# Attention on one NeuronCore: where p_low is made, and how the products for the row maxima are laid into TensorE

## The chip, the cores and the metric

One NeuronCore of one Trainium2 chip. The metric is the device time of one execution in microseconds. Engines: PE (TensorE, with PEld for its weight loads), DVE (VectorE), ACT (ScalarE), POOL (GpSimd), SP (SyncE, here the DMA queue).

## The reference

x is (2, 16, 128, 1024), that is 2 batches of 2048 tokens of 1024 channels, float32. It is group-normalized, goes through masked attention with 16 heads of 64 dimensions, 8 that look back and 8 that look ahead, and an output projection, and is added to x:

```python
def _masked_attention(xf, Wq, Wk, Wv, lookahead):
    q, k, v = (einsum('bnd,hed->bhne', xf, W) for W in (Wq, Wk, Wv))
    s = einsum('bhqe,bhke->bhqk', q, k) / sqrt(64)
    s = where(mask, s, finfo.min)        # i >= j, or i <= j for lookahead
    p = softmax(s)
    return einsum('bhqk,bhke->bhqe', p, v)
o = concatenate([o_lb, o_la], axis=1).reshape(B, T * F, D)
return x + einsum('bnd,od->bno', o, Wo)
```

## The kernel before

Float32 accuracy is had from products of the type fp32r: every operand is split in a rounded high part and a low part (the rest), and two or three products are added. A first stage, to about 1110 us, makes q, k and v of all heads (project) and stores them. The second, attend, goes over 32 heads one after the other, two (p = 0, 1) in a turn of a loop.

A head has four stages of 512 queries and 40 score tiles of 128 keys by up to 512 queries. Tiles above the diagonal are left out, so stage s has 4s full tiles and four diagonal ones of 512, 384, 256 and 128 columns. The number of such a diagonal tile modulo 4 is 0, 1, 2, 3 in that order. The shift of the softmax is a maximum over q_high times k of each query, made beforehand in 40 units (max_unit) of 128 queries by up to 512 keys, with the same counts of columns.

The order of the work is written out by hand in slots(): 40 slots a head, and each engine runs the same list and takes its own part. In slot t come: the product for the maxima of unit t+23 (of the next head past 40), the scores of tile t+3, diagonal and shift (the maxima laid on a diagonal, summed by PE into "side", copied into a row of q2), the steps of the division by the sums (invert, spread, divide, in three slots from 1, 9, 14 and 26 on), the splits of the next head's q, k and v (high parts on ACT, low parts on POOL in slots 1, 3, ... 19), the projection of the head before (8 matmuls in each of slots 9, 10, 11, 15, 16, 17), and the values of tile t.

The chain of a score tile: PE adds the products k1 q1 and k2 q2 (L1037, L1042, with a mask product L1040 on diagonal tiles) in one of two banks; ACT takes exp into probs (L859) and again, rounded, into p_high (L863); p_low = probs - p_high (L690) is made in two column parts, 3/8 on DVE and 5/8 on POOL; PE adds three products with v (L1056, L1058, L1060). probs, p_high and p_low have four buffers each. DVE makes its part of tile n-1 at the scores step of tile n. PE waits for both parts before the values, and ACT before it overwrites probs.

Partitions 0 to 63 of q1 and 64 to 127 of it both hold q_high. k1 holds k_high over k_low. k2 holds k_high in rows 0 to 63, ones in row 64 and zeros below; q2 holds q_low in rows 0 to 63 and in row 64 the shift. So k1 q1 + k2 q2 is the shifted score.

The product for the maxima (L1012) is k1 q1 over 128 rows into one of two banks by turns; PE waits until DVE has read the unit two before. DVE adds a mask to diagonal units (L921) and reduces (L927); minus_max (L932) closes a stage.

Of the kernel before, what the change touches and what calls it, by code (L numbers as in the profile page):

```python
# [5 lines left out]
F32 = mybir.dt.float32  # L6
# [26 lines left out]
def reached(eng, sem, value):  # L33

    if isinstance(value, int) and value <= 0:
        return
    eng.wait_ge(sem, value)
# [407 lines left out]
ROUND_SLOT = {("high", 0): 4, ("high", 1): 5, ("low", 0): 6, ("low", 1): 7}  # L445
OP_SLOT = {0: 9, 1: 10, 2: 11, 3: 15, 4: 16, 5: 17}
ADD_SLOT = {0: 13, 1: 19}
LOW_DVE = (3, 8)
WO_UNITS = 16
WO_SLOT = {w: 12 + 3 * w // 2 for w in range(WO_UNITS)}  # L450

# [87 lines left out]
def attend(nc, x_res, wo, qk_s, v_s, out):  # L539
    with ExitStack() as ctx:  # L540
# [135 lines left out]

        def wait_low(eng, i, p, n):

            reached(eng, low_dve, count(i, p, S_TILES, n + 1))
            reached(eng, low_pool, count(i, p, S_TILES, n + 1))  # L680

        def low_part(eng, done, kind, i, p, n):

            cols = score_tile(kind, n % S_TILES)[5]
            mine = cols * LOW_DVE[0] // LOW_DVE[1]
            part = slice(0, mine) if done is low_dve else slice(mine, cols)
            wait_high(eng, i, p, n)

            reached(eng, weighed, count(i, p, S_TILES, n - 3))
            eng.tensor_tensor(p_low[:, n % 4, part], probs[:, n % 4, part],  # L690
                              p_high[:, n % 4, part].bitcast(F32), ALU.subtract).then_inc(done, 1)
# [14 lines left out]
        def split_low(eng, p, slot, u, h):  # L706

            src = slice(h * NQ, (h + 1) * NQ)
            cols = slice((u % 2) * HALF + h * NQ, (u % 2) * HALF + (h + 1) * NQ)
            if u < 2:  # L710
                ins = eng.tensor_tensor(q2[0:E, p, cols], raw[0:E, slot, src],
                                        q1[0:E, p, cols].bitcast(F32), ALU.subtract)
            elif u < 4:
                low = k1[E:P, p, cols]
                ins = eng.tensor_tensor(low, raw[E:P, slot, src], low.bitcast(F32), ALU.subtract)  # L715
            else:
                js = slice(h * TOK // 2, (h + 1) * TOK // 2)
                ins = eng.tensor_tensor(  # L718
                    v[:, p, js, 2 * E:3 * E], raw[:, slot, src].rearrange("p (t e) -> p t e", e=E),
                    v[:, p, js, 0:E].bitcast(F32), ALU.subtract)  # L720
            ins.then_inc(low_split, 1)
# [58 lines left out]
        @block.gpsimd  # L780
        def _(pool):
            nc.gpsimd.memset(eye[:, :], 0.0).then_inc(eye_made, 1)
            nc.gpsimd.memset(below[:, :], 0.0).then_inc(eye_made, 1)
            nc.gpsimd.memset(beyond[:, :], 0.0).then_inc(eye_made, 1)
            pool.wait_ge(eye_made, 3)
            nc.gpsimd.affine_select(out=eye[:, :], in_=eye[:, :], compare_op=ALU.not_equal, fill=1.0,
                                    base=0, pattern=[[-1, P]], channel_multiplier=1).then_inc(eye_made, 1)

            nc.gpsimd.affine_select(out=below[:, :], in_=below[:, :], compare_op=ALU.is_ge, fill=MASKED,
                                    base=0, pattern=[[1, P]], channel_multiplier=-1).then_inc(consts, 1)  # L790
            nc.gpsimd.affine_select(out=beyond[:, :], in_=beyond[:, :], compare_op=ALU.is_ge, fill=MASKED,
                                    base=0, pattern=[[-1, P]], channel_multiplier=1).then_inc(consts, 1)

            pool.wait_ge(consts, 2)
            for p in range(2):
                nc.gpsimd.memset(q2[E:P, p, :].bitcast(F32), 0.0).then_inc(cleared, 1)
                nc.gpsimd.memset(k2[E:P, p, :].bitcast(F32), 0.0).then_inc(cleared, 1)  # L800
            pool.wait_ge(cleared, 4)
            for p in range(2):
                nc.gpsimd.memset(k2[E:E + 1, p, :].bitcast(F32), 1.0).then_inc(cleared, 1)
            pool.wait_ge(cleared, 6)
            for p in range(2):
                nc.gpsimd.memset(v[:, p, :, E:2 * E].bitcast(F32), 1.0).then_inc(cleared, 1)
                nc.gpsimd.memset(v[:, p, :, 3 * E:VC].bitcast(F32), 0.0).then_inc(cleared, 1)

            def do(step, kind, i, p, n):
                if step == "split low" and not first_head(i, p):  # L810

                    u, h = n // 2, n % 2
                    slot = (p * RAW_UNITS + u) % 2
                    pool.wait_ge(act_split, count(i, p, SPLITS, n + 1))


                    reached(pool, low_split, count(i, p, SPLITS, n))
                    reached(pool, low_pool, count(i, p, S_TILES, LOW_SLOT[n] + AHEAD - S_TILES + 1))
                    split_low(pool, p, slot, u, h)
                    pool.wait_ge(low_split, count(i, p, SPLITS, n + 1))  # L820
                elif step == "scores":
                    low_part(pool, low_pool, kind, i, p, n)

            heads(pool, do)

        @block.scalar
        def _(act):
            def do(step, kind, i, p, n):
                if step in ("split high", "k2 high"):
# [7 lines left out]
                    cols = slice((u % 2) * HALF + h * NQ, (u % 2) * HALF + (h + 1) * NQ)  # L837
                    if step == "k2 high":

                        nc.scalar.activation(k2[0:E, p, cols], raw[0:E, slot, src], ACT.Copy)  # L840
                    elif u < 4:
                        nc.scalar.activation((q1 if u < 2 else k1)[:, p, cols], raw[:, slot, src],
                                             ACT.Copy).then_inc(act_split, 1)
                    else:
                        js = slice(h * TOK // 2, (h + 1) * TOK // 2)
                        nc.scalar.activation(v[:, p, js, 0:E], raw[:, slot, src].rearrange(
                            "p (t e) -> p t e", e=E), ACT.Copy).then_inc(act_split, 1)
                elif step == "shift":

                    act.wait_ge(row_ready, count(i, p, STAGES, n + 1))  # L850
                    qb = n if kind == LB else STAGES - 1 - n
                    nc.scalar.activation(q2[E:E + 1, p, qb * NQ:(qb + 1) * NQ], side[E:E + 1, :],
                                         ACT.Copy).then_inc(shift_ready, 1)
                elif step == "scores":
                    cols = score_tile(kind, n)[5]
# [30 lines left out]
        def _(dve):  # L886
# [14 lines left out]
            def both_parts(kind, i, p, n):  # L901

                if n % 4 in HIGH_DVE:
# [3 lines left out]
                    reached(dve, weighed, count(i, p, S_TILES, n - 3))  # L907
                    nc.vector.tensor_copy(p_high[:, n % 4, 0:cols],
                                          probs[:, n % 4, 0:cols]).then_inc(high_dve, 1)
                low_part(dve, low_dve, kind, i, p, n)  # L910

            def do(step, kind, i, p, n):
                if step == "diagonal":
# [86 lines left out]
        def _(pe):  # L1000
            pe.wait_ge(consts, 3)

            def do(step, kind, i, p, n):
                if step == "max":
                    _, _, _, qc, key, cols, _ = max_unit(kind, n)
                    if n == 0:

                        pe.wait_ge(low_split, count(i, p, SPLITS, 8))

                    reached(pe, max_read, count(i, p, M_UNITS, n - 1))  # L1010
                    to = max_bank[n % 2]
                    nc.tensor.matmul(to[:, 0:cols], q1[:, p, qc * P:(qc + 1) * P],  # L1012
                                     k1[:, p, key:key + cols], start=True, stop=True).then_inc(max_scored, 1)
                elif step == "shift":
                    if first_head(i, p) and n == 0:

# [104 lines left out]
```

## Time and profile before

| what | value |
|---|---|
| median of 3 runs | 3432.36 us (3430.88 to 3432.69) |
| span of the profiled execution | 3431.4 us |
| PE, DVE, ACT, POOL busy | 3164.0, 2272.0, 1744.9, 1542.0 us |
| attention alone, 1300 to 3300 us: PE, DVE, ACT, POOL busy | 1862.55, 1816.54, 1425.80, 1338.35 us |

A matmul's end is modelled, and the next one begins before it: a row of 0.39 us does not mean that the next begins 0.39 us later; the starts tell the pace. The granted clock is that of TensorE, 1.00 for the full one. "Idle before" is the time that an engine stood still before an instruction, and the releaser is what ended it.

### The profile page before, as it was taken

The numbers are of one execution on the slowest core, as the hardware profiler recorded it, in microseconds if no ns is written. First come the engines' busy times: TensorE is split into PE (matmuls) and PEld (weight loads), VectorE is DVE, ScalarE is ACT, GpSimd is POOL, SyncE is SP. The second block draws the span as 40 slices with busy tenths as digits, with TensorE's granted clock in tenths as the row PEclk, the third lists the DMA queues.
The fourth block names the chain that finished last, engine by engine and source line by source line (L and its number), as shares of the span: only waits on it lengthen the run. The fifth ranks groups of instructions, "written<-read, shape, count | busy, mean of one in ns | idle before, by whom it ended". The sixth has DMA issues, their size and how long they took to land.

```text
span 3431.4 us, 53634 instructions
## 1 busy us (share of the span) xinstructions
PE 3164.0 (92%) x14472; PEld 2465.1 (72%) x14472; DVE 2272.0 (66%) x4412; ACT 1744.9 (51%) x3525; POOL 1542.0 (45%) x1626
## 2 busy tenths in 40 slices
PE   4999998999999589989999999999998999999998
PEld 3888887788888367767766677677776777767766
DVE  6212111310110599998998989998999899898996
ACT  2100101210100377777677777677777767776775
POOL 2000000100000466666666666676766666666663
PEclk9999999999999699999999999999999999999999
DMA  6234213422312222111121112111211112111210
GB/s 233 98 90 131 92 64 95 138 73 50 97 60 49 74 80 68 45 50 52 53 62 44 55 50 68 44 50 56 61 51 50 50 51 67 44 49 56 63 36 19
DMA packets 142566, 233.09 MB, mean 68 GB/s; under 512 B 76800, under 2 KB 76800, under 8 KB 142336
## 3 DMA queue, kind: packets, MB, share of 16 engines
q1 hardware_dynamic: 142336, 230.73, 22.3%
q14 instruction: 172, 1.41, 0.1%
q8 instruction: 58, 0.95, 0.1%
HBM read 163.58 MB, written 67.11 MB: 67 GB/s over the span
## 4 chain that ended last, share of the span: by engine, by line
PE 27%; DVE 13%; issue 13%; POOL 8%; ACT 4%; DMA 1%; POOLq 0%; DVEq 0%; ACTq 0%; SPq 0%
PE rows L1074 6%; POOL p_low L690 4%; PE max L1012 4%; DVE part_max L927 3%; PE scores L1042 3%; PE acc L1056 3%; PE acc L1060 3%; PE acc L1058 3%; DVE p_low L690 3%; PE scores L1037 3%; DVE o_full L981 2%; POOL k L715 2%; ACT p_high L863 2%; POOL v L718 2%; DVE inv L967 1%
## 5 line engine op out<-in xcount | busy, mean ns | idle before, releaser
L690 POOL TENSOR_TENSOR p_low<-probs,p_high 128x320 fp32r<-128x320 f32 (+3 forms) x1280 | 1072.6, 845 | 740.7 <-ACT p_high L863 678.9
L859 ACT ACTIVATE probs<-scores 128x512 f32<-128x512 f32 (+3 forms) x1280 | 686.6, 536 | 524.9 <-PE scores L1042 499.3
L927 DVE TENSOR_REDUCE part_max<-max 128x1 f32<-128x512 f32 (+3 forms) x1280 | 766.0, 599 | 83.2 <-PE max L1012 62.6
L863 ACT ACTIVATE p_high<-scores 128x512 fp32r<-128x512 f32 (+3 forms) x1280 | 685.6, 536 | 0.0
L1012 PE MATMUL max<-k,q 128*128 128x512 f32 (+3 forms) x1280 | 493.7, 387 | 164.7 <-DVE part_max L927 142.7
L690 DVE TENSOR_TENSOR p_low<-probs,p_high 128x192 fp32r<-128x192 f32 (+3 forms) x1280 | 634.2, 496 | 16.1 <-ACT p_high L863 14.2
L318 DVE COPY stage_d<-proj 128x512 f32<-128x512 f32 x96 | 66.0, 689 | 710.9 <-PE proj L264 461.1
L1042 PE MATMUL scores<-q,k 128*128 128x512 f32 (+3 forms) x1280 | 510.0, 398 | 0.0
L1056 PE MATMUL acc<-p_high,v 128*128 128x512 f32 (+3 forms) x1280 | 476.2, 372 | 9.4 <-issue 6.4
L1037 PE MATMUL scores<-q,k 128*128 128x512 f32 (+3 forms) x1280 | 475.2, 371 | 4.4 <-ACT p_high L863 4.3
L1060 PE MATMUL acc<-p_low,v 128*128 128x512 f32 (+3 forms) x1280 | 473.3, 370 | 0.0
L1058 PE MATMUL acc<-p_high,v 128*65 128x512 f32 (+3 forms) x1280 | 467.0, 365 | 0.0
L1012 PEld LDWEIGHTS max<-k,q 128*128 128x128 f32 x1280 | 247.3, 193 | 261.9 <-DVE part_max L927 203.4
L318 ACT COPY stage_a<-proj 128x512 f32<-128x512 f32 x96 | 56.0, 586 | 682.2 <-PE proj L264 359.6
L264 PE MATMUL proj<-xh,wh 128*128 128x512 f32 x896 | 348.8, 389 | 0.0
L264 PE MATMUL proj<-xh,wl 128*128 128x512 f32 x896 | 348.6, 389 | 0.0
L264 PE MATMUL proj<-xl,wh 128*128 128x512 f32 x896 | 348.6, 389 | 0.0
L1060 PEld LDWEIGHTS acc<-p_low,v 128*128 128x128 f32 x1280 | 244.9, 191 | 93.3 <-issue 5.0
L206 POOL TENSOR_TENSOR xl<-xs,xh 128x1024 fp32r<-128x1024 f32 x16 | 42.1, 2635 | 588.7 <-ACT xh L362 588.7
L1056 PEld LDWEIGHTS acc<-p_high,v 128*128 128x128 f32 x1280 | 246.5, 193 | 56.2 <-issue 18.9
L1037 PEld LDWEIGHTS scores<-q,k 128*128 128x128 f32 x1280 | 245.0, 191 | 46.1 <-ACT p_high L863 8.6
L1042 PEld LDWEIGHTS scores<-q,k 128*128 128x128 f32 x1280 | 251.7, 197 | 25.2
(94 smaller groups left out, 4981.7 us busy)
## 6 DMA issues: line engine op xcount, KB each, us to landing
raw<-qk_s SPq DMA_DIRECT2D x256, 256.0 KB, 4.2
xs<-xT SPq DMA_DIRECT2D x64, 512.0 KB, 4.8
w_raw<-wqk SPq DMA_DIRECT2D x32, 512.0 KB, 3.6
qk_s<-stage_a SPq DMA_DIRECT2D x64, 256.0 KB, 2.4
qk_s<-stage_d SPq DMA_DIRECT2D x64, 256.0 KB, 2.4
raw<-v_s SPq DMA_DIRECT2D x64, 256.0 KB, 2.8
res<-x_res SPq DMA_DIRECT2D x32, 512.0 KB, 4.1
out<-res SPq DMA_DIRECT2D x32, 512.0 KB, 2.6
```

What stands on the lines that cost most here:

```text
L264: last = nc.tensor.matmul(bank[4 * u + q][:, :], w[:, u, c, :], x[:, c, cols], start=(c == 0 and w is wh and x is xh), stop=(c == NC - 1 a ...
L690: eng.tensor_tensor(p_low[:, n % 4, part], probs[:, n % 4, part], p_high[:, n % 4, part].bitcast(F32), ALU.subtract).then_inc(done, 1)
L859: nc.scalar.activation(probs[:, n % 4, 0:cols], scores[n % 2][:, 0:cols], ACT.Exp, scale=SCALE).then_inc(exp_done, 1)
L863: nc.scalar.activation(p_high[:, n % 4, 0:cols], scores[n % 2][:, 0:cols], ACT.Exp, scale=SCALE).then_inc(high_act, 1)
L927: nc.vector.tensor_reduce(part_max[:, s % 2, at, m:m + 1], max_bank[n % 2][:, 0:cols], AX.X, ALU.max).then_inc(max_read, 1)
L1012: nc.tensor.matmul(to[:, 0:cols], q1[:, p, qc * P:(qc + 1) * P], k1[:, p, key:key + cols], start=True, stop=True).then_inc(max_scored, 1)
L1037: nc.tensor.matmul(to[:, 0:cols], k1[:, p, keys], q1[:, p, queries], start=True, stop=False)
L1042: nc.tensor.matmul(to[:, 0:cols], k2[:, p, keys], q2[:, p, queries], start=False, stop=True).then_inc(scored, 1)
L1056: nc.tensor.matmul(sums[:, col:col + cols], v[:, p, j, 0:P], high, start=first, stop=False, skip_group_check=True)
L1058: nc.tensor.matmul(sums[0:E + 1, col:col + cols], v[:, p, j, P:VC], high, start=False, stop=False, skip_group_check=True)
L1060: nc.tensor.matmul(sums[:, col:col + cols], v[:, p, j, 0:P], low, start=False, stop=final, skip_group_check=True).then_inc(weighed, 1)
L1074: last = nc.tensor.matmul(rows_bank[:, :], o[:, j, :], w[:, j, cols], start=(k == 0), stop=(k == 23))
```

## The change

p_low of a tile is made whole by one engine: by DVE for tiles with n % 4 = 3, by POOL for the others. The waits follow the counts of the one engine concerned.

q2 and k2 are turned over: k2 has ones in row 0, zeros in rows 1 to 63 and k_high in rows 64 to 127; q2 has the shift in row 0 and q_low in rows 64 to 127. The products for the maxima are issued two at a time, at even n: unit n on rows 0 to 63 (q1 and k1), unit n+1 on rows 64 to 127 (q1 and k2), each into its own bank. Their maximum is now over q_high k_high without k_low; it only shifts the softmax. PE waits before a pair until DVE has read all units up to n-1.

```diff
-LOW_DVE = (3, 8)
+LOW_DVE = (3,)
+LOW_POOL = (0, 1, 2)
...
         def wait_low(eng, i, p, n):
-            reached(eng, low_dve, count(i, p, S_TILES, n + 1))
-            reached(eng, low_pool, count(i, p, S_TILES, n + 1))
+            if n % 4 in LOW_DVE:
+                wait_one(eng, low_dve, LOW_DVE, i, p, n)
+            else:
+                wait_one(eng, low_pool, LOW_POOL, i, p, n)
         def low_part(eng, done, kind, i, p, n):
-            cols = score_tile(kind, n % S_TILES)[5]
-            mine = cols * LOW_DVE[0] // LOW_DVE[1]
-            part = slice(0, mine) if done is low_dve else slice(mine, cols)
+            part = slice(0, score_tile(kind, n % S_TILES)[5])
...
             if u < 2:
-                ins = eng.tensor_tensor(q2[0:E, p, cols], raw[0:E, slot, src],
-                                        q1[0:E, p, cols].bitcast(F32), ALU.subtract)
+                ins = eng.tensor_tensor(q2[E:P, p, cols], raw[E:P, slot, src],
+                                        q1[E:P, p, cols].bitcast(F32), ALU.subtract)
...
-                    reached(pool, low_pool, count(i, p, S_TILES, LOW_SLOT[n] + AHEAD - S_TILES + 1))
+                    wait_one(pool, low_pool, LOW_POOL, i, p, LOW_SLOT[n] + AHEAD - S_TILES)
...
-                elif step == "scores":
+                elif step == "scores" and n % 4 in LOW_POOL:
                     low_part(pool, low_pool, kind, i, p, n)
...
-                        nc.scalar.activation(k2[0:E, p, cols], raw[0:E, slot, src], ACT.Copy)
+                        nc.scalar.activation(k2[E:P, p, cols], raw[E:P, slot, src], ACT.Copy)
...
-                low_part(dve, low_dve, kind, i, p, n)
+                if n % 4 in LOW_DVE:
+                    low_part(dve, low_dve, kind, i, p, n)
...
-                if step == "max":
-                    _, _, _, qc, key, cols, _ = max_unit(kind, n)
+                if step == "max" and n % 2 == 0:
...
-                    reached(pe, max_read, count(i, p, M_UNITS, n - 1))
-                    to = max_bank[n % 2]
-                    nc.tensor.matmul(to[:, 0:cols], q1[:, p, qc * P:(qc + 1) * P],
-                                     k1[:, p, key:key + cols], start=True, stop=True).then_inc(max_scored, 1)
+                    reached(pe, max_read, count(i, p, M_UNITS, n))
+                    for m, part, keys in ((n, slice(0, E), k1), (n + 1, slice(E, P), k2)):
+                        _, _, _, qc, key, cols, _ = max_unit(kind, m)
+                        nc.tensor.matmul(max_bank[m % 2][:, 0:cols], q1[part, p, qc * P:(qc + 1) * P],
+                                         keys[part, p, key:key + cols], start=True, stop=True).then_inc(max_scored, 1)
```

The memsets of q2 and k2 and the copy of the shift move to the other rows with them.

## Rows read from the trace of the kernel before

**Rows 1.** The page's first part: busy us (share of the span) xinstructions.

```profile
PE 3164.0 (92%) x14472; PEld 2465.1 (72%) x14472; DVE 2272.0 (66%) x4412; ACT 1744.9 (51%) x3525; POOL 1542.0 (45%) x1626
```

**Rows 2.** Busy by stretch: us, PE, PEld, DVE, ACT, POOL (x), PEclk, DMA share, GB/s.

```profile
1300.00:3300.00 2000.00, 1862.55 (x8805) 1415.14 (x8804) 1816.54 (x3665) 1425.80 (x2982) 1338.35 (x1432) 0.99 0.18 53
2020.62:2037.43 16.81, 12.23 (x55) 7.69 (x53) 14.75 (x26) 12.29 (x28) 10.59 (x12) 1.00 0.12 33
2037.43:2063.32 25.89, 25.62 (x119) 20.36 (x120) 22.41 (x46) 16.31 (x34) 18.25 (x18) 1.00 0.13 41
2063.32:2091.90 28.58, 27.27 (x138) 20.83 (x137) 26.97 (x61) 21.67 (x47) 18.17 (x23) 1.00 0.26 74
...
2024.70:2041.20 16.50, 13.21 (x58) 8.45 (x57) 16.32 (x28) 12.97 (x28) 13.35 (x13) 1.00 0.12 33
```

**Rows 3.** Waits, 1300 to 3300: engine line waited for: total us, times, longest.

```profile
POOL p_low L690 <- ACT p_high L863: 565.2, 598, 3.6
...
PE max L1012 <- DVE part_max L927: 119.0, 108, 2.3
DVE max L921 <- PE max L1012: 73.8, 112, 1.6
...
ACT k L840 <- DMA raw<-qk_s: 39.1, 28, 3.0
DVE max L921 <- issue: 22.2, 10, 2.5
```

**Rows 4.** Timeline of PE, slot 31: start, us, instruction [idle before it].

```profile
2007.86 0.33 PE L1012 MATMUL max<-k,q 128*128 128x128 f32 x1 [1.32 <-DVE part_max L927]
2008.03 0.45 PE L1037 MATMUL scores<-q,k 128*128 128x512 f32 x1
2008.31 0.40 PE L1042 MATMUL scores<-q,k 128*128 128x512 f32 x1
2008.55 0.39 PE L1056 MATMUL acc<-p_high,v 128*128 128x512 f32 x1
2008.78 0.39 PE L1058 MATMUL acc<-p_high,v 128*65 128x512 f32 x1
```

**Rows 5.** The page's costliest groups: xcount | busy, mean ns | idle before, releaser.

```profile
L690 POOL TENSOR_TENSOR p_low<-probs,p_high 128x320 fp32r<-128x320 f32 (+3 forms) x1280 | 1072.6, 845 | 740.7 <-ACT p_high L863 678.9
...
L690 DVE TENSOR_TENSOR p_low<-probs,p_high 128x192 fp32r<-128x192 f32 (+3 forms) x1280 | 634.2, 496 | 16.1 <-ACT p_high L863 14.2
```

**Rows 6.** Groups by form, 1300 to 3300 us, columns as in Rows 5.

```profile
L690 POOL TENSOR_TENSOR p_low<-probs,p_high 128x320 fp32r<-128x320 f32 x802 | 762.8, 958 | 523.4 <-ACT p_high L863 497.9 <-POOL k L715 11.2 <-POOL q L711 10.3
...
L690 DVE TENSOR_TENSOR p_low<-probs,p_high 128x192 fp32r<-128x192 f32 x802 | 452.9, 565 | 0.9 <-issue 0.3
...
L981 DVE TENSOR_TENSOR o_full<-acc_s,inv 64x256 f32<-64x256 f32 x228 | 210.4, 923 | 1.5
...
L711 POOL TENSOR_TENSOR q<-raw,q 64x512 fp32r<-64x512 f32 x116 | 163.8, 1412 | 15.0 <-POOL p_low L690 9.1 <-ACT k L842 0.2 <-ACT p_high L863 0.2
L715 POOL TENSOR_TENSOR k<-raw,k 64x512 fp32r<-64x512 f32 x113 | 148.3, 1313 | 14.8 <-POOL p_low L690 9.5 <-ACT k L842 1.5
...
L718 POOL TENSOR_TENSOR v<-raw,v 128x512 fp32r<-128x512 f32 x56 | 67.2, 1200 | 7.3 <-POOL p_low L690 5.4
...
L690 POOL TENSOR_TENSOR p_low<-probs,p_high 128x80 fp32r<-128x80 f32 x115 | 41.6, 362 | 45.2 <-ACT p_high L863 33.1 <-POOL v L718 6.0 <-POOL q L711 5.3
L690 DVE TENSOR_TENSOR p_low<-probs,p_high 128x144 fp32r<-128x144 f32 x115 | 41.3, 359 | 0.0
```

**Rows 7.** Timeline of DVE before the first head: a k split, POOL idle.

```profile
1138.59 0.69 DVE L715 TENSOR_TENSOR k<-raw,k 64x512 fp32r<-64x512 f32 x1 [0.35 <-ACT k L842]
```

**Rows 8.** Timeline of DVE: p_low without and with POOL busy.

```profile
2002.55 0.34 DVE L690 TENSOR_TENSOR p_low<-probs,p_high 128x192 fp32r<-128x192 f32 x1
...
2026.19 1.45 DVE L690 TENSOR_TENSOR p_low<-probs,p_high 128x192 fp32r<-128x192 f32 x1
```

**Rows 9.** Line 690 alone, DVE's stretch A: DVE busy, POOL busy, PEclk, DMA.

```profile
2024.70:2041.20 16.50, 6.43 (x9) 7.53 (x9) 1.00 0.12 33
```

More of the change, by code:

```diff
@@ L798, in _ @@
             for p in range(2):
-                nc.gpsimd.memset(q2[E:P, p, :].bitcast(F32), 0.0).then_inc(cleared, 1)
-                nc.gpsimd.memset(k2[E:P, p, :].bitcast(F32), 0.0).then_inc(cleared, 1)
+                nc.gpsimd.memset(q2[0:E, p, :].bitcast(F32), 0.0).then_inc(cleared, 1)
+                nc.gpsimd.memset(k2[0:E, p, :].bitcast(F32), 0.0).then_inc(cleared, 1)
             pool.wait_ge(cleared, 4)
             for p in range(2):
-                nc.gpsimd.memset(k2[E:E + 1, p, :].bitcast(F32), 1.0).then_inc(cleared, 1)
+                nc.gpsimd.memset(k2[0:1, p, :].bitcast(F32), 1.0).then_inc(cleared, 1)
             pool.wait_ge(cleared, 6)
@@ L851, in do @@
                     qb = n if kind == LB else STAGES - 1 - n
-                    nc.scalar.activation(q2[E:E + 1, p, qb * NQ:(qb + 1) * NQ], side[E:E + 1, :],
+                    nc.scalar.activation(q2[0:1, p, qb * NQ:(qb + 1) * NQ], side[0:1, :],
                                          ACT.Copy).then_inc(shift_ready, 1)
```

## The prediction

> **What bounds the kernel now.** I read the busy shares first [rows 1]: PE 92%, DVE 66%. They mix two stages. The diff touches only attention, so I read the steady stretch of attention next, 1300 to 3300 us [rows 2]: PE 1862.55 of 2000 us, DVE 1816.54, POOL 1338.35. Two engines near 91 to 93% means that they take turns, and the waits say how [rows 3]: PE stands waiting for DVE's reduction of the maxima (119.0 us in 108 times, its weight loads with it), DVE at other times for PE's product (73.8 us before the mask alone), POOL 565.2 us for ACT's p_high. o_full (L981) has 8 instructions a head, and 228 of them in 2000 us are 28.5 heads: 70.2 us a head, 32 heads. The sum below is made per head. The profiled execution's span is 3431.4 us, 1.0 under the median of the runs.
>
> Within one head [rows 2] I cut at PE's products for the maxima: A, slots 1 to 8 (16.81 us), B, slots 9 to 19, which hold the output projection (25.89 us), C, slots 20 to 39 and 0 (28.58 us). One matmul of 512 columns follows another after 0.23 us [rows 4], 0.45 ns a column. Columns by score_tile and max_unit: a head has 17408 for the maxima, twice that for scores, three times for values, 24576 for the projection and 2048 for the side rows. With 0.08 us for each of 16 masked tiles (my estimate) PE needs about 9.6 us in A, 25.0 in B, 25.8 in C: 60.4 of 70.2. So PE is held up mostly in A (7.2 us), 0.9 in B, 2.8 in C. DVE also waits now and then 2.2 us for nothing that the trace shows (22.2 us in 10 times, [rows 3]), at the loop's turn: 0.8 us a head, and I keep it.
>
> **Part 1: p_low whole, a tile on one engine.** Now each tile costs one DVE and one POOL instruction: 634.2 and 1072.6 us [rows 5], 19.8 and 33.5 us a head. The diagonal tiles sit at n%4 = 0 to 3 with 512, 384, 256, 128 columns, so DVE (n%4 = 3) gets 6 tiles of 512 and 4 of 128, POOL 22 of 512, 4 of 384 and 4 of 256.
> DVE: a tile of 128 columns costs no more than the 144 columns' 0.359 us [rows 6]; no tile of 512 is there. Lower end 0.69 us, a two-input DVE instruction of 512 columns with POOL idle [rows 7]; upper end 0.69 times 0.565/0.34 = 1.15 us, the slowing that p_low of 192 columns shows beside POOL (0.34 alone, 1.45 at worst, mean 565 ns, [rows 6, 8]). I take 0.9, in between, since POOL will be busy beside it most of the time. Sum 6 x 0.9 + 4 x 0.33 = 6.7 us a head: DVE loses 13.1 us of work.
> POOL: from 80 to 320 columns it goes from 362 to 958 ns [rows 6], 2.48 ns a column. 512 columns: 1.43 us by that slope; lower end 1.20, the v split of 128 x 512. I take 1.43, the same instruction at the same contention. 384 and 256 columns: 1.12 and 0.80. Sum 31.5 + 4.5 + 3.2 = 39.2, 5.7 us more than now. With ten splits (4 x 1.412 + 4 x 1.313 + 2 x 1.200 = 13.3 us [rows 6]) and some 0.4 us of hand-over around each, 56 us a head: below the period, but dense in A.
> A rule of the skill speaks against this. The slope on POOL (2.48 ns a column, [rows 6]) is over twice DVE's (512 columns in 0.69 us, [rows 7]). The Trainium skill (GPSIMD Engine Reference, Specifications and Instruction dispatch) puts the floor for two inputs at about 2.5 cycles an element of 1.2 GHz, an estimated 1.07 us for 512 columns, and says that VectorE is the place for such work; with 1.07 POOL's sum would be 8 us smaller, and nothing below would change, since POOL is not what I count as late.
>
> Stretch A, now. DVE is busy all of 2024.7 to 2041.2: 16.32 us, 6.43 of it p_low [rows 2, 9]. The rest, 9.9, stays; p_low becomes one tile of 512 and one of 128: 1.2. That is 11.1 us plus a second of waiting: the divide lands in slot 3 (two o_full of 0.92 us each [rows 6], a transpose, a diagonal around them), and PE can't go on. Before, the product of unit n waited for the read of n-2; now a pair waits for the read of n-1, so PE is one slot ahead of DVE at a pair, not two. Step by step, from the start of slot 1, with the durations of the rows and 0.6 us for a reduce: DVE reads unit 25 by 2.7 (a reduce and the invert before it), so the pair of slot 3 starts at 2.8, where PE alone would be there at 2.4. Then come a reduce, the divide of 2.1 and unit 27 with its mask: 6.7, and the pair of slot 5 starts at 6.8 where PE would be there at 5.2. Diagonal, two reduces and one p_low of 0.9: 9.4, the pair of slot 7 at 9.5. Two reduces, a mask and two o_low: 12.3, the pair of slot 9 at 12.4. That is A: 12.4 us, with 2.8 us of waits in it. POOL has there 4 tiles of 512, one of 384, one of 256 and four q splits with hand-over: 5.7 + 1.9 + 5.6 + 1.6 = 14.8 us, but what PE needs in A is only up to tile 8, 11.3 us after A's start. So POOL is just not late. With the loop's bubble A is 13.2 us.
> B: PE's own 25.0 and 0.3 for a hiccup. POOL's later splits delay the next raw load, which already holds up ACT now and then (39.1 us in 28 times, [rows 3]); the projection's 8 matmuls in three slots cover it (1.85 us each), otherwise it would cost 1 to 2 us a head.
> C: 25.8 and a stall of 1.3 that stands there now [rows 4]: the divide in slots 26 to 28 keeps its length; p_low takes less of it, but PE has one slot less of lead. 27.1 us.
> Sum, PE's work unchanged: 13.2 + 25.3 + 27.1 = 65.6 us a head against 70.2.
>
> **Part 2: maxima two at a time.** One pair takes rows 0 to 63 and 64 to 127 of the array and two banks. If the halves run at once, a pair lasts as long as its longer unit: 768 + 2048 + 3072 + 4096 = 9984 columns a head for 17408, 0.225 us a pair where two units took 0.392, 20 pairs a head. The trace holds no matmul on 64 rows, so this is bounded: below, 0.225 and free, -0.17 us a pair; above, no overlap and a full emptying of the array on both sides of the pair. The nearest row to an emptied array is a restart after a stall: the matmul of 128 columns is followed after 0.17 us where its columns take 0.06, 0.11 us extra [rows 4]. And a matmul shows 0.39 us where the next follows after 0.23: 0.16 us of tail. I take one restart at each change of shape and no tail: 0.225 + 0.22 = 0.445, +0.05 us a pair. In A DVE hides it; 16 pairs a head pay, +0.8 us. Reduces and masks on DVE don't change. The copies that moved from the lower to the upper rows, the memsets and the constants have the same shapes: nothing.
> Before the first head, DVE reads 23 units at some 20 us in all; without the second unit in flight each of 11 pairs shows some 0.4 us more: +4 us, once.
>
> **Sum.** 65.6 + 0.8 = 66.4 us a head; (66.4 - 70.2) x 32 = -122, + 4: 3431.4 - 118 = 3314 us in the profile's time, and one more by the median. I forecast 3315.
>
> **The rivals.**
> Free switching. PE takes the columns alone: 16 x (-0.17) = -2.7, of which DVE, one slot behind, gives back 0.4: 63.3 us a head, 3216 us. For: the weight loads lie under matmuls now. Against: nothing in the trace shows it.
> The Trainium skill (TensorEngine Tiling, Theoretical Speedup) gives up to 2x for 64 rows, which is this case.
> Emptying on both sides. Tail and restart, 2 x (0.16 + 0.11) = 0.54 us, on 0.225: 0.765 for 0.392, +0.37 us a pair. A absorbs its four; 16 x 0.37 = 5.9 on 65.6 makes 71.5 us a head: (71.5 - 70.2) x 32 + 4, so 3478 us, slower. It decides from +0.28 us a pair on: below, the kernel is faster. Without overlap of the halves it is 0.17 more, 74.2 us and 3564.
> Here the Trainium skill speaks against the change as well: TensorEngine Tiling, Key Properties, says that changing the tiling mode drains TensorE, and each pair changes it twice. No run here shows the price.
> A middle of that, +0.2 us a pair: 68.8 us a head, 3392 us.
> POOL becomes the bound. If a tile costs more than 1.43 because DVE's longer instructions hold it up, A follows POOL: 14.8 + 0.8 for 13.2, 68.8 us a head, again 3392. For: POOL would have almost no gap in slots 1 to 8. Against: ring and lead of three tiles.
> The split alone does nothing: if DVE's relief were not on PE's path, 70.2 + 0.8, 3462. Against: of PE's waits that have a releaser almost all end with DVE's reduction [rows 3].
>
> **How the numbers follow.** The forecast case (3286 to 3350) 0.38; free switching (3200 to 3286) 0.27; middle or POOL (3350 to 3424) 0.17; both-sided emptying and slower cases (above 3439) 0.15; in between, near no change, 0.03. Faster by over 0.2% (about what can be told from no change) 0.82, within 0.03, slower 0.15. The range leaves out the lower tail (0.05) and the worst of the emptying (0.12): 3215 to 3450.
>
> **What would show it.** Part 1: L690 on DVE x320 near 0.75 us mean and on POOL x960 near 1.3; POOL's busy share over 50% and DVE's under 62%; PE's waits for part_max under half. If A is late by POOL, p_low on POOL stands as the releaser of acc (L1056). Part 2: the two L1012 of a pair start within some tens of ns if the halves overlap; the gap from a pair to the scores matmul, less 0.23, is the price of switching. o_full x8 a head gives the new period: 66.4 is right, 71 or more means emptying, under 64 free switching. I am wrong first of all if a 64-row matmul or its weight load has a length of its own that no row here hints at.

## The result

The changed kernel takes 3617.35 us (median of 4 runs, 3613.84 to 3618.52), the kernel before 3431.62 in the same session: 1.0542 times as long, 95% interval 1.0527 to 1.0557. That is 186 us more where the prediction had 117 less. None of its rivals reached this time; the worst of them, emptying without overlap of the halves, was 3564. Over 32 heads it is 5.8 us a head. The profiled execution's span is 3615.3 us.

The page of the kernel after, busy time by engine (to be held against [rows 1]), and busy time by stretch with the columns of [rows 2]: the steady stretch of attention, then one head cut at the pairs of slots 1, 9, 21 and 1.

```profile
PE 3299.4 (91%) x14472; PEld 2388.9 (66%) x14472; DVE 2021.0 (56%) x3452; ACT 1760.1 (49%) x3525; POOL 1644.8 (45%) x1306
```

```profile
1300.00:3300.00 2000.00, 1849.77 (x8206) 1253.64 (x8205) 1472.13 (x2612) 1337.69 (x2764) 1330.18 (x1064) 0.96 0.17 50
...
2031.90:2046.56 14.66, 11.27 (x54) 7.21 (x53) 14.03 (x21) 11.46 (x25) 11.91 (x10) 1.00 0.12 36
2046.56:2074.81 28.25, 27.98 (x125) 20.00 (x126) 19.39 (x36) 18.66 (x36) 20.06 (x18) 1.00 0.13 39
2074.81:2107.00 32.19, 28.00 (x132) 18.37 (x132) 22.19 (x43) 20.21 (x44) 18.74 (x16) 0.99 0.22 65
```

DVE did lose its work: 1472 us of 2000 where it had 1816.54 [rows 2], and its 30 instructions fewer a head. But PE is no less busy, it does fewer heads in the time (8206 matmuls for 8805), and DVE, with time to spare, now waits for PE too. The waits, with the columns of [rows 3], and the groups by form, with those of [rows 6]:

```profile
DVE part_max L929 <- PE max L1014: 341.1, 287, 3.1
PEld max L1014 <- DVE part_max L929: 242.2, 244, 3.0
PE max L1014 <- DVE part_max L929: 143.2, 104, 2.5
```

```profile
L691 POOL TENSOR_TENSOR p_low<-probs,p_high 128x512 fp32r<-128x512 f32 x588 | 784.1, 1344 | 617.2 <-ACT p_high L864 563.6 <-PE acc L1062 36.3 <-POOL k L716 6.1
...
L983 DVE TENSOR_TENSOR o_full<-acc_s,inv 64x256 f32<-64x256 f32 x214 | 226.9, 1060 | 2.9 <-issue 1.5
...
L691 DVE TENSOR_TENSOR p_low<-probs,p_high 128x512 fp32r<-128x512 f32 x161 | 151.0, 938 | 0.0
```

PE waits for the reduction of the maxima more than before (143.2 us for 119.0), although DVE has less to do: two engines that wait for each other, neither full. 214 o_full are 26.75 heads in 2000 us, 74.8 us a head for 70.2.

The pair itself stands in the timeline of PE and, below it, of PE's weight loads, the kernel after, slot 13 and its neighbours (start, us):

```profile
2056.45 0.40 PE L1060 MATMUL acc<-p_high,v 128*65 128x512 f32 x1
2056.69 0.40 PE L1062 MATMUL acc<-p_low,v 128*128 128x512 f32 x1
2057.01 0.50 PE L1014 MATMUL max<-k,q 64*128 64x512 f32 x2
2057.44 0.51 PE L1039 MATMUL scores<-q,k 128*128 128x512 f32 x1
2057.78 0.40 PE L1044 MATMUL scores<-q,k 128*128 128x512 f32 x1
```

```profile
2056.45 0.19 PEld L1062 LDWEIGHTS acc<-p_low,v 128*128 128x128 f32 x1
2057.01 0.19 PEld L1014 LDWEIGHTS max<-k,q 64*128 64x128 f32 x2 [0.37 <-issue]
2057.44 0.19 PEld L1039 LDWEIGHTS scores<-q,k 128*128 128x128 f32 x1 [0.24 <-issue]
2057.55 0.19 PEld L1044 LDWEIGHTS scores<-q,k 128*128 128x128 f32 x1
```

Both products are one row with 0.50 us: they start within a hundredth of a microsecond of each other and run at once. Around them time is lost. A matmul of 512 columns is followed after 0.23 us elsewhere; here the pair starts 0.32 us after the last values matmul (0.09 more), the scores matmul 0.43 us after the pair (0.20 more), and the next 0.34 us after that (0.11 more). From the starts in the timeline from 1300 to 2300 us the medians are 0.10 (136 pairs without another wait), 0.43 (213) and 0.11 (120). The weight loads show the same places: the load of the last values matmul starts 0.24 us ahead of it (2056.45 for 2056.69), but the load of the 64-row products starts with them, and so does that of the first 128-row product behind them. A pair of full units costs 0.64 us where two products cost 0.46. Three gaps, some 0.40 us, stand against 7424 columns saved in 20 pairs, 0.17 us each.

### The profile page after: what moved, and what is told of

It is laid out like the page before. It is cut to its first block, busy times and chain, and to the rows that moved or that the text cites. A ratio compares the mean times of both kernels' runs of the same rounds, so it can differ in the third digit from the quotient of the medians.

```text
span 3615.3 us, 50218 instructions
## 1 busy us (share of the span) xinstructions
PE 3299.4 (91%) x14472; PEld 2388.9 (66%) x14472; DVE 2021.0 (56%) x3452; ACT 1760.1 (49%) x3525; POOL 1644.8 (45%) x1306
## 4 chain that ended last, share of the span: by engine, by line
PE 32%; POOL 12%; DVE 11%; issue 10%; ACT 1%; DMA 0%; POOLq 0%; DVEq 0%; SPq 0%; ACTq 0%
POOL p_low L691 6%; PE scores L1039 6%; PE max L1014 5%; PE rows L1076 5%; PE scores L1044 4%; PE acc L1062 4%; PE acc L1058 4%; PE acc L1060 4%; DVE part_max L929 3%; POOL k L716 3%; DVE p_low L691 3%; POOL q L712 2%; DVE o_full L983 2%; DVE inv L962 1%; DVE inv L969 1%
## 5 line engine op out<-in xcount | busy, mean ns | idle before, releaser
L691 POOL TENSOR_TENSOR p_low<-probs,p_high 128x512 fp32r<-128x512 f32 (+2 forms) x960 | 1168.1, 1230 | 831.8 <-ACT p_high L864 754.1
L1039 PE MATMUL scores<-q,k 128*128 128x512 f32 (+3 forms) x1280 | 554.4, 433 | 2.5 <-ACT p_high L864 2.3
L1014 PE MATMUL max<-k,q 64*128 64x512 f32 (+3 forms) x1280 | 327.0, 478 | 233.1 <-DVE part_max L929 201.7
L1044 PE MATMUL scores<-q,k 128*128 128x512 f32 (+3 forms) x1280 | 524.0, 409 | 0.0
L1062 PE MATMUL acc<-p_low,v 128*128 128x512 f32 (+3 forms) x1280 | 484.2, 378 | 0.0
L1060 PE MATMUL acc<-p_high,v 128*65 128x512 f32 (+3 forms) x1280 | 477.0, 373 | 0.0
L1014 PEld LDWEIGHTS max<-k,q 64*128 64x128 f32 x1280 | 123.6, 190 | 460.8 <-DVE part_max L929 325.7
L1039 PEld LDWEIGHTS scores<-q,k 128*128 128x128 f32 x1280 | 250.3, 196 | 176.7 <-issue 119.8
L1058 PEld LDWEIGHTS acc<-p_high,v 128*128 128x128 f32 x1280 | 253.8, 198 | 41.1 <-POOL p_low L691 2.2
L983 DVE TENSOR_TENSOR o_full<-acc_s,inv 64x256 f32<-64x256 f32 x256 | 269.2, 1051 | 3.6 <-issue 1.8
L1044 PEld LDWEIGHTS scores<-q,k 128*128 128x128 f32 x1280 | 260.6, 204 | 9.6
```

The lines of the kernel that those rows point to most:

```text
L983: last = nc.vector.tensor_tensor(o_full[a * E:(a + 1) * E, :, rows], sums, by, ALU.mult)
L1014: nc.tensor.matmul(max_bank[m % 2][:, 0:cols], q1[part, p, qc * P:(qc + 1) * P], keys[part, p, key:key + cols], start=True, stop=True).the ...
L1039: nc.tensor.matmul(to[:, 0:cols], k1[:, p, keys], q1[:, p, queries], start=True, stop=False)
L1044: nc.tensor.matmul(to[:, 0:cols], k2[:, p, keys], q2[:, p, queries], start=False, stop=True).then_inc(scored, 1)
L1058: nc.tensor.matmul(sums[:, col:col + cols], v[:, p, j, 0:P], high, start=first, stop=False, skip_group_check=True)
L1060: nc.tensor.matmul(sums[0:E + 1, col:col + cols], v[:, p, j, P:VC], high, start=False, stop=False, skip_group_check=True)
```

## The experiments

Four kernels take the change apart. Theories: S, the changes of the array's shape cost, from 128 rows to 64 for the products for the maxima and back; L, PE's lost lead costs: before a pair DVE must have read both banks, so PE can't be two slots ahead; P, whole tiles cost. A ratio is to the kernel before, measured again in the same session.

**The split alone.** The changed kernel with the products of before:

```diff
-                if step == "max" and n % 2 == 0:
+                if step == "max":
...
-                    reached(pe, max_read, count(i, p, M_UNITS, n))
-                    for m, part, keys in ((n, slice(0, E), k1), (n + 1, slice(E, P), k2)):
...
+                    reached(pe, max_read, count(i, p, M_UNITS, n - 1))
+                    to = max_bank[n % 2]
+                    nc.tensor.matmul(to[:, 0:cols], q1[:, p, qc * P:(qc + 1) * P],
+                                     k1[:, p, key:key + cols], start=True, stop=True).then_inc(max_scored, 1)
```

> Part 1 alone: p_low whole tiles on one engine as in the changed kernel, but the products for the maxima one at a time over 128 rows, waiting for the read of n-2. Theory S (the shape of the array is what costs: 0.63 us for a pair of 64-row products with its surroundings where two 128-row products take 0.46, so some 4 to 5 us a head): this kernel is faster than before, 65.6 us a head by the prediction's own sum, 3285 us, at any rate under 3400. Theory L (what costs is that PE is only one slot ahead of DVE at a pair): also under 3400. Theory P (whole tiles on POOL cost: DVE's o_full beside a 512-column POOL instruction rose from 0.92 to 1.05 us and to 1.5 at worst): at or above 3431.

Measured 3390.11 us, 0.9881 of before (0.9865 to 0.9898): 41 us faster, 1.3 us a head. P falls, S and L stand, and the gain is under a third of the 4.6 us a head (147 us) that the sum had for this part. Stretch, waits and groups of the kernel with the split alone, 1300 to 3300 us:

```profile
1300.00:3300.00 2000.00, 1922.07 (x9013) 1423.89 (x9012) 1661.62 (x2869) 1462.97 (x3045) 1481.99 (x1172) 1.00 0.19 54
```

```profile
PEld acc L1058 <- POOL p_low L691: 28.2, 47, 0.9
...
PEld acc L1058 <- DVE p_low L691: 26.6, 30, 0.9
...
PE max L1014 <- DVE part_max L929: 16.6, 40, 1.3
...
ACT k L841 <- DMA raw<-qk_s: 134.6, 58, 2.7
```

```profile
L691 POOL TENSOR_TENSOR p_low<-probs,p_high 128x512 fp32r<-128x512 f32 x648 | 884.7, 1378 | 475.9 <-ACT p_high L864 440.0 <-PE acc L1062 15.3 <-POOL k L716 12.5
...
L1058 PE MATMUL acc<-p_high,v 128*128 128x512 f32 x825 | 341.3, 414 | 29.8 <-POOL p_low L691 16.3 <-DVE p_low L691 13.6
...
L983 DVE TENSOR_TENSOR o_full<-acc_s,inv 64x256 f32<-64x256 f32 x234 | 249.1, 1064 | 3.3 <-issue 1.8
...
L691 DVE TENSOR_TENSOR p_low<-probs,p_high 128x512 fp32r<-128x512 f32 x177 | 196.5, 1110 | 10.6 <-ACT p_high L864 8.9 <-PE acc L1062 1.8
```

PE's wait for the maxima falls from 119.0 to 16.6 us, and the values wait for p_low of both engines in its place. DVE's other instructions beside POOL got slower, o_full from 923 [rows 6] to 1064 ns. ACT waits 134.6 us for the raw loads where it waited 39.1 [rows 3], which the prediction had expected of POOL's later splits; in the two and two below, with less on POOL, it is 37.8. Whether this wait reaches PE no run tests.

**The pairs alone.** The changed kernel with p_low in column parts of 3/8 and 5/8 and their waits, as before the change:

```diff
-LOW_DVE = (3,)
-LOW_POOL = (0, 1, 2)
+LOW_DVE = (3, 8)
...
```

> Part 2 alone: p_low in column parts of 3/8 and 5/8 as before, the products for the maxima two at a time over 64 rows. Theories S and L: slower than before, at least 3580, and since DVE is as loaded as before, slower than the changed kernel (above 3617). Theory P: near 3431 to 3500, under the changed kernel.

Measured 3610.64 us, 1.0514 (1.0496 to 1.0531). At least 3580, as S and L said; P wrong. But the two also had it above the changed kernel, and that it is not: it is 7 us under it, and the intervals of the two (1.0527 to 1.0557 for the changed one) overlap. Under the pairs the split's 41 us are gone.

**Pairs over all 128 rows.**

```diff
-                    for m, part, keys in ((n, slice(0, E), k1), (n + 1, slice(E, P), k2)):
+                    for m, part, keys in ((n, slice(0, P), k1), (n + 1, slice(0, P), k1)):
```

> The changed kernel with both products of a pair over all 128 rows of q1 and k1: no change of the array's shape, nothing at once, the pair's wait (read of n-1) kept. Theory S: the gap of 0.09 before and 0.20 and 0.11 us after the pair goes, 2 x 0.23 stay; 20 pairs x 0.17 to 0.23 us are 3.4 to 4.6 us a head, so 3617 - 110 to 150 = 3470 to 3510, and less if the clock is granted in full. Theory L: the wait stays, so the time stays, 3600 or more.

Measured 3490.18 us, 1.0172 (1.0155 to 1.0189). S's forecast came, L's (3600 or more) did not, and yet both have a part: the shape is 3617 - 3490 = 127 us, 4.0 us a head, and 3490 - 3390 = 100 us, 3.1 a head, stay against the split alone. Between those two kernels only the pair differs: both products issued together at the even slot, behind one wait for both banks. The waits of this kernel:

```profile
DVE part_max L929 <- PE max L1014: 269.1, 275, 2.9
PEld max L1014 <- DVE part_max L929: 231.1, 253, 2.7
PE max L1014 <- DVE part_max L929: 128.5, 123, 2.3
```

From 16.6 to 128.5 us, with the same work on every engine as in the split alone.

**64-row products one at a time**, in the lower and upper half by turns, each waiting for the read of n-2:

```diff
+                    reached(pe, max_read, count(i, p, M_UNITS, n - 1))
+                    part, keys = ((slice(0, E), k1), (slice(E, P), k2))[n % 2]
```

> The changed kernel with its 64-row products one at a time, by turns in the lower and the upper half, each waiting for the read of n-2: the shape changes 80 times a head in place of 40, and PE is two slots ahead of DVE again. Theory S: 0.40 us of surroundings for each of 40 products and nothing at once: some 12 us a head more PE work than before, above 3800. Theory L: the lead is back, under the changed kernel's 3617.

Measured 3696.53 us, 1.0777 (1.0759 to 1.0795): 306 us over the split alone. S is right in sign and too high by 100 us, L wrong for this kernel. Timeline of PE around a 64-row product of 512 columns and one of 128, and the wait:

```profile
2002.82 0.39 PE L1062 MATMUL acc<-p_low,v 128*128 128x512 f32 x1
2003.14 0.50 PE L1014 MATMUL max<-k,q 64*128 64x512 f32 x1
2003.57 0.50 PE L1039 MATMUL scores<-q,k 128*128 128x512 f32 x1
...
2006.44 0.40 PE L1062 MATMUL acc<-p_low,v 128*128 128x512 f32 x1
2006.77 0.32 PE L1014 MATMUL max<-k,q 64*128 64x128 f32 x1
2007.03 0.49 PE L1039 MATMUL scores<-q,k 128*128 128x512 f32 x1
```

```profile
PE max L1014 <- DVE part_max L929: 1.2, 4, 0.4
```

One product alone is followed after 0.43 us, as a pair is: the second half comes free. With 128 columns it is 0.26 us, 0.06 and the same 0.20. So the cost belongs to the change of shape, not to the 64-row product's length or to the pair: 0.4 us for going there and back, for one product or two, of 128 columns or 512. Whether three or more 64-row products in a row would pay it only once, no run shows. Forty times a head that is 16 us, and only 9.6 show, because the slower PE hides waits that the split alone has. PE hardly waits for DVE's reduction any more (1.2 us in 2000 for 16.6), but that is the smaller part: by the count of gaps below, made for this kernel too, what goes is 1.4 us a head before the maxima, 1.8 before and within the values, 1.3 before the side product and the projection, and the rest in the scores. S had forgotten that.

**Giving the lead back.** In the changed kernel and in the one with pairs over 128 rows DVE now reads both units at the even step:

```diff
+                elif step == "max" and n % 2 == 0:
+                    read_unit(kind, i, p, n)
+                    read_unit(kind, i, p, n + 1)
                 elif step == "max":
...
+                    pass
```

> The changed kernel, but DVE reads both units of a pair one after the other at the even step, so that at the next pair PE may be up to two slots ahead of DVE again. Nothing else. Theory L (the lead of one slot costs the 3.1 us a head by which the kernel with pairs over 128 rows, 3490, is over the one with the split alone, 3390): most of 100 us comes back, 3510 to 3540. Rival C (not the lead, but that a pair comes as a burst and DVE stands before it): no change, 3600 to 3620.

Measured 3513.53 us, 1.0252 (1.0233 to 1.0271): 104 us back, as L said.

> The kernel with pairs over all 128 rows, with the same edit: DVE reads both units at the even step. Theory L: from 3490 back to near the split alone, 3390 to 3410. Rival C: stays at 3490. The difference between the run before this one and this one is the price of the array's shape without the lost lead: theory S says 3.9 to 4.7 us a head, 125 to 150 us.

Measured 3450.69 us, 1.0063 (1.0046 to 1.0080): 40 us back, not 80 to 100. So the lead is a cause in both (C falls), but DVE's order is not that of the split alone, and 60 us remain; how much of them is that order and how much the pair no run separates. The starts of PE's matmuls show where most of it is, in the table below: the side product now waits 1.6 us a head for a diagonal, which comes behind two reductions, and 1.6 us more stay before the maxima. And between these two kernels the shape costs 63 us, not 127. The table puts the difference before the maxima: with one slot of lead the gap there is 2.2 us a head longer with 64 rows than with 128 (8.4 for 6.2), which is the 2.0 of the change of shape and nothing hidden; with the lead back it is only 0.8 longer (4.1 for 3.3), so the slower PE hides 1.2 us of its wait for DVE. Why it hides nothing in the first case no kernel here tells.

To compare kernels I took all starts of PE's matmuls in the timeline from 1800 to 2368 us and gave 0.451 ns to each column (0.04 us to a mask product); what is left before a matmul is a gap. In us a head, heads counted by the tiles:

```
                        before  split alone  pairs 128  changed  changed, lead back  pairs 128, lead back
a head                   69.7      68.2        71.0      75.0          71.9                 69.3
columns                  59.7      59.7        60.3      56.5          56.1                 60.1
gap before the maxima     4.8       1.7         6.2       8.4           4.1                  3.3
gap behind the maxima     0.9       1.1         0.9       4.5           4.3                  0.2
gap within the scores     0.5       0.6         0.7       2.7           2.6                  0.5
gap before the values     1.7       2.6         1.5       1.4           1.7                  1.7
all others                2.2       2.5         1.5       1.5           3.2                  3.4
```

Columns fall by 3.2 to 4 us with 64-row pairs, the gaps behind the maxima and within the scores rise by 5.8, and 2.0 (20 x 0.10) of the gap before the maxima is the same change of shape.

**Two and two.** Since in the split alone both engines' p_low had come late:

```diff
-LOW_DVE = (3,)
-LOW_POOL = (0, 1, 2)
+LOW_DVE = (1, 3)
+LOW_POOL = (0, 2)
```

> The split alone (128-row products one at a time) with the whole tiles n%4 = 1 and 3 on DVE and 0 and 2 on POOL. In the split alone PE's waits for the maxima fell by 3 us a head, and some 1.5 us of waits of the values for p_low came in their place. Theory V (those are POOL's: three 512-column tiles of 1.38 us in a row beside its splits): they go, and if DVE's extra 8 to 10 us a head fit in its idle time, 3350 to 3385. Rival D (DVE is full again in slots 1 to 8): the waits for the maxima return, 3410 to 3450.

Measured 3402.62 us, 0.9919 (0.9903 to 0.9936), 12 us behind the split alone and in neither forecast. V had the direction of the values' waits for p_low right (2.9 us of PE in 2000 for 29.9), but in the kernel's waits DVE is late again, as D said, though less than before the change:

```profile
PE max L1014 <- DVE part_max L929: 93.5, 53, 2.8
```

**A quarter of the columns.** The kernel before with one number changed:

```diff
-LOW_DVE = (3, 8)
+LOW_DVE = (1, 4)
```

> The kernel before with the column parts of p_low at 1/4 on DVE and 3/4 on POOL in place of 3/8 and 5/8: the same share of the work as in the split by whole tiles, but still one instruction on each engine for every tile. Theory W (the gain of the split alone, 41 us, comes from DVE's 30 instructions fewer a head, since a p_low of 128 columns still costs 0.35 to 0.45 us): DVE loses 40 x 0.15 = 6 us a head here in place of 13, POOL gets 6 more; PE's waits for the maxima fall by about half as much, 3405 to 3425. Rival X (only the share counts): 3385 to 3395. Rival Y (a POOL part of 384 columns, 1.05 us, in every tile makes the values wait): 3430 or more.

Measured 3433.18 us, 1.0006 (0.9996 to 1.0015): no change, in the range that Y had. Rival X falls; what whole tiles gave is not the share of the columns. The relief of DVE that W counted on did not come: its busy time in the stretch is 1834.07 us, before 1816.54. The group by form of this kernel, to be held against the 192 columns of [rows 6], and its waits:

```profile
L690 DVE TENSOR_TENSOR p_low<-probs,p_high 128x128 fp32r<-128x128 f32 x803 | 510.1, 635 | 0.9 <-issue 0.3
```

```profile
PE max L1012 <- DVE part_max L927: 79.9, 99, 1.9
...
PE acc L1056 <- DVE p_low L690: 20.4, 48, 0.7
...
PE acc L1056 <- POOL p_low L690: 8.4, 19, 0.6
```

128 columns cost DVE 635 ns, more than 192 did (565); POOL's part beside them is longer, 384 columns for 320. With POOL idle the same 128 columns take 0.28 us (the changed kernel, at 2075.95 us). So a small DVE part doesn't get cheap while POOL works beside it, and each one pays by itself; 30 fewer of them a head is the reading of the gain that is left, and the two and two, with 20 fewer, gained 27 us. It is not shown alone: POOL has ten instructions fewer too, and each tile then waits for one engine. Nor does POOL's length explain all, since o_full here took 844 ns, less than the 923 before. PE's waits for the maxima did fall, from 119.0 to 79.9 us, but those of the values for p_low rose from 1.9 to 28.8 us, as Y said, though by the trace more for DVE's part than for POOL's, and the two cancel.

**The clock.** Behind PE's long waits the granted clock falls to half. The kernel after at the loop's turn, PE's timeline, and windows of 4 us (window, us, busy PE, PEld, DVE, ACT, POOL, granted clock, DMA share, GB/s):

```profile
2104.32 0.40 PE L1062 MATMUL acc<-p_low,v 128*128 128x512 f32 x1
2107.00 0.80 PE L1014 MATMUL max<-k,q 64*128 64x512 f32 x2 [2.28 <-DVE part_max L929]
2107.72 0.79 PE L1039 MATMUL scores<-q,k 128*128 128x512 f32 x1
2108.32 0.63 PE L1044 MATMUL scores<-q,k 128*128 128x512 f32 x1
```

```profile
2104.00:2108.00 4.00, 1.72 (x6) 0.76 (x5) 1.33 (x4) 1.54 (x5) 1.35 (x2) 0.82 0.02 6
2108.00:2112.00 4.00, 4.00 (x12) 2.91 (x12) 2.82 (x6) 2.73 (x6) 1.61 (x2) 0.50 0.00 0
```

Summed over all windows of 4 us from 1300 to 3300 us (twice what is missing to 1.00) PE is at 1.2 GHz for 58 us before the change, 143 after it, 75 with pairs over 128 rows, 24 and 20 with the lead given back, and not at all in the split alone. That looks like a cause of its own, so I filled the wait with matmuls that nobody reads:

```diff
+                    if p == 0 and n == 24:
...
+                        reached(pe, added, count(i, p, 2, -2))
+                        for _ in range(8):
+                            nc.tensor.matmul(rows_bank[:, :], q1[:, p, 0:P], k1[:, p, 0:NQ],
+                                             start=True, stop=True)
```

> The changed kernel with eight extra 128-row matmuls (512 columns, into the projection's bank, which is free there, read by nobody) on PE before the wait of the pair of slot 1 in every second head, where PE stands 2.3 us at the loop's turn and the granted clock then is 0.50 for some 6.5 us. They are 1.85 us of work in a wait of 2.3. Theory K (the lost clock is a part of the change's loss: such a stretch costs about half its length): with 16 turns and some 3.2 us each the kernel is up to 50 us faster than 3617, 3565 to 3600, and the mean granted clock from 1300 to 3300 us rises from 0.96. Rival N (the clock costs nothing, because DVE is late anyway): same time within 10 us, or slower by what the filling delays.

Measured 3606.38 us, 1.0507 (1.0485 to 1.0529). The time at half clock in the profiled execution fell from 143 to 75 us in 2000, as much as pairs over 128 rows have, and the kernel got 11 us faster where half the length of those stretches would be some 40. The 11 us are themselves uncertain: the five runs spread from 3596.54 to 3616.89, and the interval touches that of the changed kernel. Its stretch:

```profile
1300.00:3300.00 2000.00, 1854.30 (x8359) 1257.91 (x8359) 1480.58 (x2624) 1343.80 (x2779) 1333.19 (x1068) 0.98 0.17 50
```

The same in the kernel before, six matmuls at n == 25:

> The kernel before with six such extra matmuls before the product of unit 25 in every second head, 1.4 us of work where PE stands 1.6 us at the loop's turn. Its granted clock is at half for about 58 of the 2000 us from 1300 on. Theory K: up to 30 us faster than before, 3400 to 3425, most of what the split alone gained (3390, with no half clock at all). Rival N: same within 7 us, or slower.

Measured 3430.33 us, 1.0001 (0.9992 to 1.0010); but here the filling hardly raised the clock (51 us at half for 58), so this run says little. The kernel with a quarter of the columns says more: by the same sum it is at half clock for 10 us where the kernel before is for 58, in the same time. By the first of these runs the clock is worth some 10 us of the loss, between K and N and nearer to N. That DVE sets the pace right behind the loop's turn, so that a slow PE only waits less, fits this and is not shown.

No version tried beats the split alone, 3390.11 us, 1.2% under the kernel before.

## Why the prediction was wrong

It summed three terms; two had the wrong size and one was hardly there. In us a head:

| step | forecast | shown by | measured |
|---|---|---|---|
| DVE's relief by whole tiles | -4.6, with the pairs' wait in it | split alone against before | -1.3 |
| the pair waits for the read of n-1, both products at once | some of A and C, no term of its own | pairs over 128 rows against split alone | +3.1 |
| change of shape, 64 rows | +0.8 | changed against pairs over 128 rows | +4.0 |
| sum | -3.8 | | +5.8 |

The measured terms are differences in this order of steps. The relief and the pairs don't simply add: the pairs alone cost 5.6 us a head, and the split on top of them gives nothing back. Giving the lead back returns 1.2 us a head with pairs over 128 rows and 3.2 in the changed kernel.

**"DVE loses 13.1 us of work"** was too high. In the split alone its p_low took 8.1 us a head (236.4 us in 29.25 heads), not 6.7, because a tile of 512 cost 1.11 us and not 0.9. What the step left out is that POOL's longer instructions slow DVE's others: 8 o_full by 0.14 us, two o_low by 0.25, four diagonals by 0.09, some 2 us a head. Relief 10 us by the durations, not 13, and by the busy time in the stretch only 7, from 63.7 to 56.8 us a head (1816.54 us over 28.5 heads, 1661.62 over 29.25): rows of DVE overlap, and a small p_low's duration counted in full time that it shared with its neighbours. The prediction's sum had counted durations too.

**"So POOL is just not late"** failed. Of the 3.1 us a head that PE's gap before the maxima lost in the split alone, 0.9 came back before the values and 0.6 at other places. POOL's prices were right (1.38 us for 1.43, 37.5 us a head for 39.2); that a tile is ready one slot in time on average was not enough, and the same went for DVE's own whole tile, which the step hadn't looked at.

**"PE is one slot ahead of DVE at a pair, not two"** was seen, and stepped through in A only, where 12.4 us became 14.66 with the bubble standing elsewhere. In B and C it was given 0.3 and nothing. C, slots 20 to 0, was to be 27.1 us; slots 21 to 0 alone are 32.2, with ten pairs in them and two stops of 1.9 and 2.3 us before a pair. PE stands before a pair even where DVE has spare time in sum, because DVE's work comes in bursts and one slot is 1.3 us: the first stop ends a stretch in which DVE does two o_full (1.92 us) and a p_low beside POOL (1.73 us), and the second, at the loop's turn, follows 2.36 us in which DVE waits for nothing that the trace shows.

**"One restart at each change of shape and no tail", +0.05 us a pair**, was the wrong choice between its bounds. Measured are 0.10 before, 0.20 and 0.11 behind, 0.41 in all for the 0.22 taken: a pair of the average kind costs 0.225 + 0.41 = 0.64 us for 0.392, +0.24. The rival had +0.37 (0.54 of emptying). The mechanism of that rival is the one that the rows bear out, gaps on both sides of the pair, and the size lies between. The Trainium skill (TensorEngine Tiling, Key Properties) says that a change of the tiling mode drains TensorE: the runs agree, with about 0.4 us for a change and back. The rule of its section Theoretical Speedup, up to 2x, holds for the products themselves, which start together, and not for a pair between 128-row matmuls. The Trainium skill (TensorE: Matmul & The Clock Gate, Part 2) has weight loads pulled ahead of matmuls in flight; at a change of shape the rows show none pulled ahead (both start at 2057.01, and again at 2057.44).

The break-even of +0.28 us a pair in the prediction was right only with the relief of 4.6. With 1.3 it would have been +0.08, and with the pair's wait nothing was left: pairs over 128 rows, which change no shape, are already slower than before.

What held: DVE's and POOL's columns and counts, DVE's share under 62% (it is 56%; POOL's, which was to be over 50%, stayed at 45%, and at 49% in the split alone), both halves at once, and the few us more before the first head: from the first product for the maxima to the first scores it takes 30.5 us for 25.1. That the copies moved to other rows cost nothing no run tests alone.

## What to carry over

Cost a change of two parts as two changes, and ask of each wait that it moves how many steps one engine may be ahead of the other afterwards: here two products at once behind a wait for both banks cost 3.1 us a head without one instruction more. Products on half of the array's rows must save more columns than the change of shape costs: each product or pair among full ones costs about 0.4 us here, as much as 900 columns. Larger groups may pay it once; no run here has them. A relief is worth what the next wait leaves of it, so look at what comes late second before counting the first.

## What the runs showed of the hardware

- Two 64-row products in the two halves start within a hundredth of a microsecond of each other; the next 128-row matmul starts 0.43 us behind them (512 columns) for 0.23, and the same behind one alone. Behind one of 128 columns it is 0.26 us for 0.06.
- A DVE instruction with two operands in SBUF can get longer as it gets smaller: p_low of 128 columns took 635 ns on average beside POOL parts of 384 columns, of 192 columns beside 320 columns 565 ns, and of 128 columns with POOL idle 0.28 us.
- Of 68 us fewer at half clock in 2000 the changed kernel gained only 11 us in its whole time (medians; the runs spread over 20 us).
